# A two-slot ring in the hop sum and three load slots in layer 1's projection, with the normalised rows computed again instead of stored

## What is computed

```python
x = x + L0_gnn(layernorm(x), src, dst, ...)              # gives x1
x = x + L0_ffn(layernorm(x)[None], ..., edge_index)[0]   # gives x2
# in L0_ffn: a hop attention over 65536 edges makes scores for 4 experts
#   agg = segment_sum(h[src] * alpha[:, :, None], dst)   # the hop sum
#   w = softmax(top_k(layernorm(agg).mean(heads), 2))    # the gate
#   out = sum over e of g[e] * (gelu(x @ W1[e] + b1[e]) @ W2[e] + b2[e])
x = x + L1_gnn(layernorm(x), edge_index, edge_attr, ...)
# in L1_gnn: xp = x @ W; attention over the edges;
#   y = x + out + bias, with x the normalised input; layernorm(y) * gamma + beta
x = x + L1_ffn(layernorm(x)[None], ...)[0]               # 8 experts, softmax weights
```

## Time and profile before

| | us |
|---|---|
| median of 3 runs | 7137.76 |
| lowest and highest | 7133.32, 7147.25 |
| the profiled execution | 7156.78 |
| its span, first to last instruction | 7154.9 |

### The profile page before, as it was taken

How to read it: one execution, slowest core, us unless ns; L and a number is a source line. 1 busy time by engine, 2 the same in 40 slices (tenths; PEclk the granted TensorE clock), 3 DMA queues, 4 the chain that set the end, 5 groups by cost and what they waited for, 6 DMA issues and landing times. The chain is left out here.

```text
span 7154.9 us, 86877 instructions
## 1 busy us (share of the span) xinstructions
PE 4895.2 (68%) x21453; PEld 3505.2 (49%) x21454; DVE 3944.3 (55%) x9373; ACT 2616.2 (37%) x5007; POOL 3190.5 (45%) x3260
## 2 busy tenths in 40 slices
PE   4468366777777778378877753354555556999999
PEld 3246134555555578345555453333344334666565
DVE  4257136899888966312221287466666666444443
ACT  0134004555555533033333331355555553222222
POOL 2641605677777657356666400466666661000000
PEclk6568797899989965588888856677777777999999
DMA  2001257788888877233333207555555553000000
GB/s 50 1 0 39 52 166 223 235 244 247 245 241 244 242 178 173 81 89 74 80 82 77 76 3 235 184 145 144 148 146 145 147 145 101 16 15 15 15 15 11
DMA packets 616359, 852.88 MB, mean 119 GB/s; under 512 B 209716, under 2 KB 419611, under 8 KB 615645
## 3 DMA queue, kind: packets, MB, share of 16 engines
q0 software_dynamic: 159136, 383.90, 20.7%
q1 hardware_dynamic: 319069, 416.84, 18.5%
q10 hardware_dynamic: 137972, 50.36, 3.0%
HBM read 692.81 MB, written 164.74 MB: 120 GB/s over the span
## 5 line engine op out<-in xcount | busy, mean ns | idle before, releaser
L1340 POOL DMA_INDIRECT b_got<-tmp_l_table,b_src x928 | 998.7, 1076 | 445.6 <-issue 263.8
L2444 POOL DMA_INDIRECT w_got<-tmp_l_table,w_src x928 | 878.9, 947 | 539.4 <-issue 247.7
L3158 POOL DMA_INDIRECT t_got<-tmp_f_table,t_src x672 | 634.0, 943 | 429.7 <-DVE t_sums L3236 224.2
L2693 PE MATMUL w_pa<-w_got,w_hot 128*128 128x264 f32 x1856 | 639.7, 503 | 204.1 <-issue 106.5
L1586 PE MATMUL b_pk<-b_keys,b_hot_t 128*128 x1856 | 549.4, 447 | 290.7 <-issue 179.8
L2693 PEld LDWEIGHTS w_pa<-w_got,w_hot 128*128 128x128 f32 x1856 | 436.9, 248 | 321.3 <-issue 226.6
L1586 PEld LDWEIGHTS b_pk<-b_keys,b_hot_t 128*128 128x128 f32 x1856 | 386.5, 219 | 379.3 <-issue 320.6
L3617 DVE SCALAR_TENSOR_TENSOR l_accs<-l_po,l_prob,l_accs 128x256 f32 (+1 forms) x392 | 173.5, 480 | 598.4 <-PE l_po L3723 598.4
L1601 PE MATMUL b_pa<-b_got,b_hot 128*128 128x260 f32 x1856 | 485.8, 408 | 6.7 <-issue 2.5
L3668 ACT ACTIVATE l_h<-l_ph,l_bn 128x896 f32<-128x896 f32 x224 | 245.0, 1096 | 661.9 <-PE l_ph L3713 661.9
L3272 PE MATMUL t_ph<-t_xt,t_w 128*128 128x448 f32 x896 | 406.5, 599 | 110.5 <-issue 110.4
(11 more groups left out here) (570 smaller groups left out, 9993.9 us busy)
## 6 DMA issues: line engine op xcount, KB each, us to landing
tmp_g_acc<-b_acc SPq DMA_DIRECT2D x232, 260.0 KB
w_spread<-tmp_g_rel_rows SPq DMA_DIRECT2D x232, 256.0 KB
t_spread<-tmp_f_rel_rows SPq DMA_DIRECT2D x170, 256.0 KB
b_spread<-tmp_g_rel_rows SPq DMA_DIRECT2D x116, 256.0 KB
e_attr<-in_edge_attr ACTq DMA_DIRECT2D x103, 256.0 KB
tmp_f_experts<-t_y SPq DMA_DIRECT2D x28, 896.0 KB
yl_y<-tmp_f_experts SPq DMA_DIRECT2D x28, 896.0 KB, 10.9
b_got<-tmp_l_table,b_src POOLq DMA_INDIRECT x928
```

Of the source, the lines that this page charges most:

```text
L1340: pool.indirect_dma_start(out=got[:, m % NB, u, :], out_offset=None, in_=T["l0_table"], in_offset=bass.IndirectOffsetOnAxis(ap=src[:, m * ...
L2444: pool.indirect_dma_start(out=got[:, p % 3, u, :], out_offset=None, in_=T["l1_table"], in_offset=bass.IndirectOffsetOnAxis(ap=src[:, p * R ...
L2693: mm = pe.matmul(pa[:, (k * RS + n) % SUMS, 0:WV], hot[:, (k * B4 + b) % 3, u - b * U, :], got[:, k, u, 0:WV], start=(u == 2 * n), stop=(u ...
L3158: pool.indirect_dma_start(out=got[:, g % DEPTH, u, :], out_offset=None, in_=T["f_table"], in_offset=bass.IndirectOffsetOnAxis(ap=src[:, g ...
```

## The change

1. In the hop sum `parts` becomes a ring of two pieces. ACT's loop is written out; from the third piece on it waits until PE has summed the piece before last. PE's and DVE's index into the parts comes from the position in the loop's body instead of from the loop's register.
2. `FirstLoads` is made before the hop sum, and `loads.first` is issued there by SP, ahead of its wait for `last_ready`. Once the hop sum's memory is free a third slot is made, and the gate's SP stream loads chunk 2 into it.
3. The projection uses three slots: after chunk c's x2 it loads chunk c + 3. It stores no normalised rows; DVE no longer waits for that store. SP's and DVE's loops are written out.
4. The last stage loads x2 alone and normalises it again: seven bn_stats and seven bn_aggr in `attended`, a root on ACT (behind layer 0 of expert 3), and a reciprocal and seven tensor_scalar in `added`.

The diff, cut to its core:

```diff
+class Statistics:
+    def take(self, dve, link, x):
+        for t in range(TPC):
+            ins = dve.bn_stats(self.stat[:, t, :], x[:, t, :])
+        link.done(ins)
+        dve.nop(nofuse=True)
+        for t in range(TPC):
+            ins = dve.bn_aggr(self.mv[:, t, :], self.stat[:, t, :])
+        ins.then_inc(self.var_ready, 1)
+    def root(self, act, K, c):
+        act.wait_ge(self.var_ready, c + 1)
+        act.activation(self.sd[:, :], self.mv[:, :, 1], ACT.Sqrt, bias=K["eps"][:, 0:1]).then_inc(self.sd_ready, 1)
+    def scale(self, dve, link, c, x, out):
+        dve.wait_ge(self.sd_ready, c + 1)
+        link.done(dve.reciprocal(self.rstd[:, :], self.sd[:, :]))
+        for t in range(TPC):
+            ins = dve.tensor_scalar(out[:, t, :], x[:, t, :], self.mv[:, t, 0:1], self.rstd[:, t:t + 1],
+                                    ALU.subtract, ALU.mult)
...
 def stage_hop_sum
-        parts = s.sb("parts", [P, L.steps, 3, Q], BF16)
+        parts = s.sb("parts", [P, 2, PIECE * TURN, 3, Q], BF16)
...
             sp.dma_start(stop_i[:, :], T[L.name + "_i_row"][0:L.stops].partition_broadcast(P)).then_inc(stops_in, 16)
+            loads.first(sp, T)
             sp.wait_ge(last_ready, 1)
...
-            with act.Fori(0, PIECES) as p:
+            for p in range(PIECES):
+                if p >= 2:
+                    act.wait_ge(summed, 2 + (p - 1) * PIECE)
                 for k in range(3):
                     act.wait_ge(left_ready, 3 * p + k + 1)
-                    part = piece_of(parts, p)[:, :, k, :]
+                    part = parts[:, p % 2, :, k, :]
...
-                                       parts[:, bass.ds(t * TURN + h * U + u, 1), :, :].rearrange("p a k q -> p (a k q)"),
+                                       parts[:, at // PIECE % 2, at % PIECE * TURN + h * U + u, :, :].rearrange("p k q -> p (k q)"),
...
 def stage_hop_gate
-            loads.first(sp, T)
+            loads.chunk(sp, T, 2)
...
 def stage_l1_project
-            def front(c, h=None):
+            def front(c):
                 sp.wait_ge(x2_ready, c + 1)
                 sp.dma_start(chunk_of(T["x2"], c), n.x[:, :, :]).then_inc(x2_stored, 16)
-                if h is not None:
-                    loads.chunk(sp, T, c + 2, h)
-                sp.wait_ge(n.xn_ready, c + 1)
-                sp.dma_start(chunk_of(T["l1_xn"], c), n.xn[:, :, :]).then_inc(xn_stored, 16)
+                if c + 3 < CHUNKS:
+                    loads.chunk(sp, T, c + 3)
...
-            front(0, 0)
-            with sp.Fori(0, CHUNKS // 2 - 1) as i:
-                for h in range(2):
-                    front(2 * i + h + 1, 1 - h)
-                    back(2 * i + h)
-            for c in (CHUNKS - 3, CHUNKS - 2):
+            front(0)
+            for c in range(CHUNKS - 1):
                 front(c + 1)
                 back(c)
...
-                dve.wait_ge(xn_stored, 16 * c)
                 dve.wait_ge(n.turned, c)
                 n.vector(dve, link, c).then_inc(n.xn_ready, 1)
...
 def stage_l1_finish_and_experts3
-        x2 = z.sb("x2", [P, TPC, D])
+        x2 = m.x
+        before = Statistics(z)
...
-                m.load(sp, T["l1_xn"], c)
-                sp.dma_start(x2[:, :, :], chunk_of(T["x2"], c)).then_inc(m.x_loaded, 16)
+                m.load(sp, T["x2"], c)
...
             def attended(c):
+                dve.wait_ge(m.x_loaded, 16 * (c + 1))
+                before.take(dve, link, x2)
...
             def added(c):
-                dve.wait_ge(m.x_loaded, 32 * (c + 1))
-                link.done(dve.tensor_tensor(sum_[:, :, :], sum_[:, :, :], m.x[:, :, :], ALU.add))
+                link.done(before.scale(dve, link, c, x2, m.xn))
+                link.done(dve.tensor_tensor(sum_[:, :, :], sum_[:, :, :], m.xn[:, :, :], ALU.add))
...
+                    if more and (layer, e) == (0, 3):
+                        before.root(act, K, c + 1)
                     if more and (layer, e) == (0, E // 2):
                         m.scalar(act, K, c + 1)
```

More of the change, by code:

```diff
@@ L2753, in _, with stage_hop_sum @@
             round_(58, 1, False, False, True)
-def stage_hop_sum(nc, T, K, weight, rows, acc):
+def stage_hop_sum(nc, T, K, weight, rows, acc, loads):
     L, H, W = HOP, 4, 16
@@ L2851, in prepare @@
                 else:
-                    part = piece_of(parts, p)[:, :, k - 1, :]
+                    part = parts[:, at % 2, :, k - 1, :]
                     dve.wait_ge(part_ready, 3 * p + k)
@@ L2936, in __init__, with third, chunk @@
         self.loaded = s.sem("loaded")
[L2937 to L2940 removed]
+        self.chunk_in = [s.sem(f"chunk_in{h}") for h in range(3)]
+        self.x1_of = [self.x1[:, h, :, :] for h in range(2)]
+        self.y_of = [self.y[:, h, :, :, :] for h in range(2)]
+    def third(self, nc, ctx):
+        s = Scope(nc, ctx, "yt")
+        self.x1_of.append(s.sb("x1", [P, TPC, D])[:, :, :])
+        self.y_of.append(s.sb("y", [P, self.E, TPC, D])[:, :, :, :])
+    def chunk(self, sp, T, c):
+        h = c % 3
+        sp.dma_start(self.x1_of[h], chunk_of(T["x1"], c)).then_inc(self.chunk_in[h], 16)
         for e in range(self.E):
[L2942 removed]
+            sp.dma_start(self.y_of[h][:, e, :, :], chunk_of(T["f_experts"][e], c)).then_inc(self.chunk_in[h], 16)
     def first(self, sp, T):
[L2945 removed]
+        self.chunk(sp, T, 0)
         sp.dma_start(self.w[:, :, :], T["L1_gnn_W"].rearrange("(a p) n -> p a n", p=P)).then_inc(self.loaded, 16)
@@ L3301, in stage_l1_project @@
         n = Norm(s)
-        w, att, gate, x1, y = loads.w, loads.att, loads.gate, loads.x1, loads.y
+        w, att, gate = loads.w, loads.att, loads.gate
         loaded, chunk_in = loads.loaded, loads.chunk_in
@@ L3349, in _ @@
             sp.wait_ge(stored, 16)
-            for sem in (x2_stored, xn_stored, row_stored):
+            for sem in (x2_stored, row_stored):
                 sp.wait_ge(sem, 16 * CHUNKS)
@@ L3365, in _, with front @@
             ins.then_inc(w_att_ready, 1)
-            def front(c, h, turn):
-                dve.wait_ge(chunk_in[h], 16 * (1 + E) * (turn + 1))
-                link.done(dve.tensor_copy(mine[:, :, :], gate[:, bass.ds(c * TPC, TPC), :]))
+            def front(c):
+                h = c % 3
+                x1, y = loads.x1_of[h], loads.y_of[h]
+                dve.wait_ge(chunk_in[h], 16 * (1 + E) * (c // 3 + 1))
+                link.done(dve.tensor_copy(mine[:, :, :], gate[:, c * TPC:(c + 1) * TPC, :]))
                 dve.wait_ge(x2_stored, 16 * c)
@@ L3373, in front @@
                     for t in range(TPC):
-                        ins = dve.scalar_tensor_tensor(n.x[:, t, :], y[:, h, e, t, :], mine[:, t, e:e + 1],
-                                                       x1[:, h, t, :] if e == 0 else n.x[:, t, :], ALU.mult, ALU.add)
+                        ins = dve.scalar_tensor_tensor(n.x[:, t, :], y[:, e, t, :], mine[:, t, e:e + 1],
+                                                       x1[:, t, :] if e == 0 else n.x[:, t, :], ALU.mult, ALU.add)
                     link.done(ins)
                 dve.sem_inc(x2_ready, 1)
-                dve.wait_ge(xn_stored, 16 * c)
                 dve.wait_ge(n.turned, c)
                 n.vector(dve, link, c).then_inc(n.xn_ready, 1)
-            front(0, 0, 0)
-            with dve.Fori(0, CHUNKS // 2) as i:
-                link.loop(i, 2 * (1 + E + 2))
-                for h in range(2):
-                    front(2 * i + h + 1, 1 - h, i + h)
-            link.leave(CHUNKS // 2)
+            for c in range(CHUNKS):
+                front(c)
         @block.scalar
@@ L3624, in _ @@
             with dve.Fori(0, CHUNKS - 1) as c:
-                link.loop(c, 2 + 4 + 1 + E + 11)
+                link.loop(c, 2 + 4 + 1 + E + 11 + 3)
                 for e in range(E):
@@ L3644, in _ @@
         def _(act):
+            before.root(act, K, 0)
             m.scalar(act, K, 0)
@@ L3814, in two_layers @@
             stage_softmax(nc, T, K, HOP, 4, 1.0, score)
-            with held("hop_sums", [P, NODE_TILES, 16 + 4]) as sums:
-                stage_hop_sum(nc, T, K, score, rows, sums)
-                with ExitStack() as held_loads:
-                    loads = FirstLoads(nc, held_loads)
-                    stage_hop_gate(nc, T, K, sums, loads)
-                    stage_l1_project(nc, T, K, loads)
+            with held("hop_sums", [P, NODE_TILES, 16 + 4]) as sums, ExitStack() as held_loads:
+                loads = FirstLoads(nc, held_loads)
+                stage_hop_sum(nc, T, K, score, rows, sums, loads)
+                loads.third(nc, held_loads)
+                stage_hop_gate(nc, T, K, sums, loads)
+                stage_l1_project(nc, T, K, loads)
         with held("l1_sums", [P, NODE_TILES, D + 8]) as sums:
```

33 lines of the change are left out of this document (17 added, 16 removed).

## The result

The changed kernel takes **7116.5 us** in the median (7104.6 to 7125.6, 10 runs) against 7138.0 us (7121.4 to 7147.3, 10 runs) of the kernel before on the same chip: 21.5 us less, ratio 0.9971, 95% interval 0.9960 to 0.9981. That is 0.3% less (interval 0.2 to 0.4%); 8 us less had been forecast, within 0.2%. Its profiled execution took 7107.9 us (span 7106.0), one of its shortest, where the profiled one of before (7156.8) was longer than any of these runs. A difference of the two spans, 48.9 us, therefore says nothing; the stages have to be compared one by one.

A forecast was written before the change was run, and what follows sets the result against it. DVE was taken to bound the hop sum, gate and projection, PE the last stage. Terms -3.1 (hop sum), 0 (loads), -8.4 (projection), +3.2 (last stage) summed to -8.3 us: 7129.5 us median, range 7118 to 7144.

The forecast's parts named there:

- Hop sum, -3.1: Hop sum: static index makes looped turns as fast as the last piece; DVE's 3.1 us of waits for PE go.
- ACT's ring wait, 0: Hop sum: ACT's added wait for PE's sums of the piece before last is already met when reached; cost 0.
- Loads moved, 0: First loads issued in the hop sum, not the gate: nothing saved or lost, 0 us; bounds -0.2 to +1.
- Projection, wait for the stored rows, -10.9: Layer 1's projection: DVE's 12.0 us of waits in 5 chunks go, except 0.22 us each; -10.9 us.
- x2 waits: Projection: a chunk's first sum waits for the previous chunk's x2 store; 0 to 2.7 us, 0.5 taken.
- Projection, PE's last chunk, +2: Projection's end: PE's last chunk may get a lower clock than before; 0 to +4.4 us, +2 taken.
- Last stage, start, +3.2: Before PE's first matmul: 5.7 us of DVE work added, parameters landing 2.5 us sooner; +3.2 us (+1.3 to +5.7).
- Expert loop, 0: Last stage's six chunks: added DVE work and ACT's root stay covered, one table load moved; cost 0.
- rival 1: Everything falls well: no x2 store waits, fast last PE chunk, parameters 4.4 us sooner; -12.7 us, 7125.1 us; chance 0.20.
- Rivals 2, 3 and 4: 2: x2 queue, slow PE, 7136.6, 0.15; 3: PE stays low, 7166.6, 0.05; 4: ring doesn't speed PE, 7132.6, 0.10.

The follow-up runs named there:

- rows on ACT: Whole change, plus each row's mean and 1/deviation kept in memory and ACT writing the projection's normalised rows from two x2 buffers; 6250.5 us against 6276.0 before, ratio 0.9962.

## Why the prediction was wrong

The range ended at 7118; the median was 7116.5. Point by point:

- **Hop sum, -3.1: right in kind, small by 1.1.** 163.1 to 158.9 us, in the ring-only kernel too. The 3.1 us of waits for PE are gone, but "only DVE's waits for PE count" was too narrow: DVE's idle time over the whole stage fell by 3.4 us (5.3 to 1.9), since its two waits for ACT's first parts shrank too (1.5 to 1.2). The remaining 0.8 isn't idle time of DVE, and no row explains it. The upper bound of 3.3 was drawn from a window that didn't cover the stage.
- **ACT's ring wait, 0: right.** No row has ACT waiting for PE in the hop sum.
- **Loads moved, 0: right, for the wrong question.** Gate 25.7 for 26.0. The working asked what the early loads save (nothing) and not what the third chunk would cost without them: 12.0 us.
- **Projection, wait for the stored rows, -10.9: right.** It is gone; DVE's part lost 11.1 us against 10.4 forecast (-10.9 + 0.5). In its parts: idle time before the statistics 12.4 to 1.0 us over seven chunks (the 0.22 that was to stand is 0.15), 0.6 from the written-out loop, which was put at 0, and 1.0 us of x2 waits in 2 chunks for 0.5, inside its 0 to 2.7. That seven transfers per 18.1 us are "just balanced" held: 354 and 356 GB/s in the two chunks from 4380.59 to 4416.30, 17.85 us each. The estimate from the Trainium skill, DMA: Bandwidth & Descriptors, section Where 436 GB/s comes from, of 18.1 us for such a chunk agrees within 0.3 us. What the prediction drew from it, that the loading chunks can't be shorter "whatever is saved", did not hold: with the rows on ACT, DVE took 15.7 us for a chunk while the engines moved 330 to 359 GB/s, since with three slots DVE doesn't wait for the chunk being loaded.
- **Projection, PE's last chunk, +2: wrong.** It compared with one execution that happened to have the fast clock. In the first pair of traces it looks right (+1.3), by luck: over all traces the median tail is 23.4 us without and 22.4 with the change, each within a spread of 5 us. The term is 0, or a little less.
- **Last stage, start, +3.2: right.** +2.8 from SP's first load, +3.2 from the stage's first instruction, ACT's table load (work +5.6, wait 2.4 shorter).
- **Expert loop, 0: right.** 1119.3 for 1120.0 us; one table load of 1.28 us, moved as said. The Trainium skill's 2.66 us (ScalarE: Activation LUTs, section What ACT_TABLE_LOAD costs) includes a drain that no row here shows.

The touched stages therefore give -12.2 us in the first pair of traces, and -14.0 by the medians of all traces (-4.3 hop sum, -11.0 DVE's part, -1.0 tail, +2.8 start, -0.5 experts), where the sum had -8.3. On the chips near 6275 us that is what was measured (-12.0 and -15.1). It is near rival 1's price of -12.7, to which 0.20 was given, but not by its route: the x2 waits came, and the parameters landed 2.4 us sooner and not 4.4.

**The failed steps** are two. The first is in the sum: the terms for the hop sum (-3.1) and for PE's last chunk (+2) were mis-sized; they measured -4.3 and -1.0 over the traces, which with smaller differences makes the touched stages' gain 4 to 6 us larger. By that alone the median would be 7124 to 7126 us, inside the range of 7118 to 7144. The second took the median out of the range: stages outside the diff were put at 0, with 7 us for spread, and in the first result another 7 to 9 us lie there. What brings them stays open; the four comparisons on chips above 7000 us all have such an excess, those near 6275 us have none, and the same kernel timed twice differed by as much once.

Rivals 2, 3 and 4 have no trace: x2 waits of 1.0 us, a PE that spent part of each chunk at the high level (granted 0.71 to 0.88 in the seven chunks of the first trace with the change, 0.62 to 1.00 in the others), and weight loads at 1.08 us.

## What to carry to other kernels

A tail at the end of a stage that hangs on TensorE's clock should be priced from several executions, or not at all: one profile's tail of 21.1 us was one of ten between 20.7 and 26.4. Before an edit adds transfers to a stage, ask not only who waits for the data but whether the issuing engine gets through before the stage's end: behind four to six unfinished transfers each 896 KB load held SyncE for 2.5 to 3.0 us, and 12 us of that came onto the path. And where two chips differ in a stage by 20%, look on each for the engine that sets its pace before an edit's gain is carried from one to the other; an unchanged kernel in the same set is the measure of what is noise.

## What the runs showed of the hardware

- Sixteen pairs of weight load (128x128 bf16) and matmul (60 columns) took 2.20 us where the matmul's operand `parts` was indexed by a loop register, and 1.08 us with a constant index, at the same granted clock of 0.50. The weight load reads `hot`, whose index is constant in both. The trace has a register instruction of 55 ns ahead of each pair in the first case and none in the second; most pairs follow each other at 134 ns in the first case, at 62 ns in the second. DVE's loop cost 0.10 us a chunk in the projection (0.13 against 0.03 us ahead of its first sum).
- The same kernel takes 7083 or 6275 us, by the chip, at granted clocks of 0.80 and 0.83. The long differences lie in stages with indirect transfers (edges of layer 1: 1439 and 1199 us, hop scores and experts about 1055 and 869), though layer 0's edge stage, with as many gathers, differs by 2% (about 1473 and 1439). Of the stages without, the experts take 1119 to 1122 us on all, softmax 84.4 to 85.8 and the hop sum 158.8 to 159.0 with the ring.
- POOL issued a gather in 0.95 us and the next 0.30 us later, so 928 of them bound a stage at 1168 us where nothing else held it.
- On the slower kind of chip the order of waits in layer 1's edge loop settled in one of two patterns, by kernel as far as seen: the same in all four traces of the kernel before and in both of each of the two kernels that were traced twice there.
